# Reordering VectorE's steps in the loop body of a two-layer transformer block: three moves in a table

## The reference

```
x = x + L0_attn(layernorm(x))   # linear attention, 16 heads: phi(q) (phi(k)^T v) Wo, phi = silu + 1
x = x + L0_ffn(layernorm(x))    # 256 -> 2 x 1024, silu gate; 1024 -> 1024 gelu; 1024 -> 1024 gelu; 1024 -> 256
x = x + L1_attn(layernorm(x))   # softmax attention, one head of 256
x = x + L1_ffn(layernorm(x))    # three 256 x 256 products, tanh(h + bias)
```

## Time and profile before

| | |
|---|---|
| median of 3 runs | 2006.14 us (2004.3 to 2007.96) |
| the profiled execution's own time | 2003.38 us |
| its span, first to last instruction | 2001.6 us |
| mean granted clock of TensorE | 0.998 of full speed |
| PE busy | 1914.8 us, 96% of the span |
| DVE busy | 1340.3 us, 67% |
| ACT busy | 782.9 us, 39% |
| POOL busy | 397.6 us, 20% |

### The profile page before, as it was taken

The page is one execution under the profiler, slowest core; times in us unless marked ns, Lnnn a source line. Parts: engine busy times, 40 slices in busy tenths (PEclk is TensorE's granted clock), DMA queues, the critical chain, the costliest instruction groups (busy, mean ns, idle before and its releaser), DMA issues.

```text
span 2001.6 us, 27379 instructions
## 1 busy us (share of the span) xinstructions
PE 1914.8 (96%) x10170; PEld 1634.2 (82%) x10170; DVE 1340.3 (67%) x3183; ACT 782.9 (39%) x1258; POOL 397.6 (20%) x344
## 2 busy tenths in 40 slices
PE   8999999999999999999999999999999999999998
PEld 6888787887878888788787887878788787887886
DVE  6676686766757577676776766758666686765347
ACT  3443434343343433434334343343433434343333
POOL 1212030221302113021130311303022030220211
PEclk9999999999999999999999999999999999999999
DMA  9531312313022130221303113031231312213200
GB/s 370 176 105 43 122 37 74 106 43 137 22 81 99 53 137 22 87 83 53 137 32 106 53 65 125 32 117 42 76 114 43 122 37 74 106 43 127 81 15 23
DMA packets 59241, 171.10 MB, mean 85 GB/s; under 512 B 5296, under 2 KB 25520, under 8 KB 58928
## 3 DMA queue, kind: packets, MB, share of 16 engines
q1 hardware_dynamic: 59104, 169.25, 24.4%
HBM read 160.85 MB, written 19.92 MB: 90 GB/s over the span
## 4 chain that ended last, share of the span: by engine, by line
PE 74%; DVE 16%; ACT 6%; issue 3%; DMA 0%; ACTq 0%; POOL 0%; DVEq 0%
PE ffn_fill L1152 33%; PE att_fill L1083 23%; PE ffn_fill L1083 12%; DVE turned L801 5%; PE ffn_fill L1205 4%; DVE turned_b L818 3%; DVE act_lo L840 2%; DVE xn L720 2%; ACT whole L1013 1%; ACT act_hi L1015 1%; PE att_fill L1283 1%; DVE sm L908 1%; DVE prob_t_lo L903 1%; ACT L1044 1%; ACT L1013 1%
## 5 line engine op out<-in xcount | busy, mean ns | idle before, releaser
L1152 PE MATMUL ffn_fill<-act_hi,hw 128*128 128x512 f32 x2048 | 804.1, 393 | 0.0
L1152 PE MATMUL ffn_fill<-act_lo,hw 128*128 128x512 f32 x2048 | 798.6, 390 | 0.0
L1152 PEld LDWEIGHTS ffn_fill<-act_lo,hw 128*128 128x128 f32 x2048 | 384.7, 188 | 76.7
L1152 PEld LDWEIGHTS ffn_fill<-act_hi,hw 128*128 128x128 f32 x2048 | 384.6, 188 | 76.7
L840 DVE TENSOR_TENSOR act_lo<-whole,act_hi 128x512 fp32r<-128x512 f32 x256 | 177.0, 691 | 280.4 <-ACT act_hi L1015 279.5
L1013 ACT ACTIVATE whole<-ffn_fill,scales 128x512 f32<-128x512 f32 x256 | 175.9, 687 | 467.5 <-PE ffn_fill L1152 467.2
L681 POOL TENSOR_TENSOR act_lo<-whole,act_hi 128x512 fp32r<-128x512 f32 x128 | 166.4, 1300 | 299.9 <-DVE act_hi L836 299.3
L1083 PE MATMUL ffn_fill<-half_hi,w 128*128 128x512 f32 x512 | 203.6, 398 | 2.8 <-DVE wz_lo L946 2.7
L1083 PE MATMUL ffn_fill<-half_lo,w 128*128 128x512 f32 x512 | 200.6, 392 | 0.0
L1015 ACT ACTIVATE act_hi<-whole 128x512 fp32r<-128x512 f32 x256 | 161.7, 631 | 8.2
L818 DVE STREAM_TRANSPOSE turned_b<-xn_b 32x128 f32<-32x128 f32 x480 | 145.1, 302 | 6.6
(11 more groups left out here) (242 smaller groups left out, 3167.5 us busy)
## 6 DMA issues: line engine op xcount, KB each, us to landing
hw<-scratch_h1T SPq DMA_DIRECT2D x128, 512.0 KB, 3.3
hw<-scratch_h2T SPq DMA_DIRECT2D x128, 512.0 KB, 3.2
x<-in_L_attn_x SPq DMA_DIRECT2D x16, 512.0 KB, 4.0
out<-x SPq DMA_DIRECT2D x15, 512.0 KB, 4.0
w<-scratch_w1T SPq DMA_DIRECT2D x1, 1024.0 KB, 8.9
w<-scratch_w2T SPq DMA_DIRECT2D x1, 1024.0 KB, 11.0
w<-scratch_w3T SPq DMA_DIRECT2D x1, 1024.0 KB, 8.5
rows<-in_rows SPq DMA_DIRECT2D x1, 640.0 KB, 5.7
```

What stands on the lines that cost most here:

```text
L1152: last = pe.matmul(bank[:], view(hw[:, j, k, :]), view(moving[:, k, :]), start=k == 0 and half == 0, stop=k == KH - 1 and half == 1)
```

## The change

Three steps change their place in DVE's table for the body. No other engine's table is touched, no instruction is added or removed, and the tables of the first and the last stage stay.

```diff
     "BODY": order_from("""
-         a:AST H5 a:ANO a:Ta H6 a:Tb H7 W0 W1 c:CSTa U0 a:AKV0 U1 a:AKV1 c:CSTb U2 a:AKV2 U3 a:AKV3 U4 U5 a:AS
+         a:AST H5 a:ANO a:Ta H6 H7 a:Tb W0 W1 c:CSTa U0 a:AKV0 U1 a:AKV1 c:CSTb U2 a:AKV2 U3 a:AKV3 U4 U5 a:AS
     a:AQ U6 a:AM U7 c:CNO a:AO n:BST0 c:LT c:CQ G0 n:BST1 c:CV G1 c:CZ c:CS0 G2 c:CS1 c:CP0 c:CS2 c:CO0 c:CP1
-    c:CS3 G3     c:CO1 c:CP2 G4 c:CO2 c:CP3 n:BNO0 c:CO3 c:DSTa c:DSTb G5 c:DNO n:NT0a G6 n:NT0b c:LT G7 n:NTL0
+    c:CS3     c:CO1 c:CP2 G3 G4 c:CO2 c:CP3 n:BNO0 c:CO3 c:DSTa c:DSTb G5 c:DNO n:NT0a G6 c:LT n:NT0b G7 n:NTL0
     n:BNO1     c:CF H0 n:NT1a H1 n:NT1b H2 n:NTL1 H3 H4"""),
```

## The result

| | before | after |
|---|---|---|
| median, device us | 2005.23 (4 runs, 2004.3 to 2007.96) | 1947.22 (4 runs, 1946.51 to 1949.3) |
| ratio to before, 95% interval | | 0.971 [0.9693, 0.9727] |
| the profiled execution's own time | 2003.38 | 1946.51 |
| its span | 2001.6 | 1944.8 |
| mean granted clock | 0.998 | 0.997 |

The account below looks back on a forecast made before the run. TensorE was busy 96%, so time could come only from its idle gaps: 1.2 + 0.63 + 2.05 = 3.9 us in each of 14 passes, 54 us, giving 2006.1 - 54 = 1952 us; range 1938 to 1967.

Parts of the forecast that it names:

- Site 3: CF's wait for LT's low half: LT ahead of NT0's second half removes it, 2.05 us a pass.
- the cover: At H0's last eighth: G7's delayed low half is still ready 0.64 us before TensorE loads its weights.
- Site 2: CO2's wait for prob_t_lo: G3 behind CO1 and CP2 saves 0.63 us a pass; ACT's high half ends the rest.
- the upper bound of the prediction: At CO2: 1.42 us a pass if ACT's high half were not in the way.
- Site 1: W0's wait for H7's low half: H7 ahead of the second transposes removes 1.92 us, of which 1.2 is kept.
- the prediction's other branch: At line 850: DVE's addition goes between POOL's two instructions, AKV0 loads 0.74 late, 1.08 us is kept.
- debt in the U steps: DVE, held up by POOL, starts U0 only 0.43 us earlier and stays behind TensorE up to AS.
- the test that the prediction names: DVE's start of U0: at 1126 or earlier its first rival holds; beyond 1128 W0's gain is given back.
- its first rival: W0's gain is kept whole, DVE's addition coming up 0.1 us before POOL: 4.6 us a pass, 1942 us, 15%.
- Line 850's longest: Expected sign on DVE: the longest run of W's addition to x stretches to nearly 3 us.

Follow-up runs that it names:

- e4: Changed kernel with G7's low half moved further back on DVE, behind NTL0, BNO1 and CF's evictions; 1952.48 us.
- Move 3 alone: Kernel before with only the second LT moved ahead of NT0's second half on DVE; 1974.74 us.
- e9: Kernel before with H7 ahead of the second transposes, G3's low half behind CO1 and CP2, and 14 unused TensorE products ahead of CF's wait; 1976.98 us.
- e6: Kernel before with H7 ahead of the second half of the transposes and 14 unused TensorE products ahead of CF's wait; 1985.31 us.
- e8: Changed kernel with ACT making CP2's and CP3's high halves ahead of G3's and G4's activations, DVE's table following; 1936.55 us.
- its control: Kernel before, its order kept, with the same 14 unused TensorE products ahead of CF's wait; 2005.16 us.
- e10: Changed kernel with W's result scaled in place in PSUM and added to x from there, in two instructions with one SBUF operand each; 1941.27 us.
- move 1 alone: Kernel before with only H7 moved ahead of the second half of the transposes on DVE; 2003.29 us.
- move 2: Kernel before with only G3's low half moved behind CO1 and CP2 on DVE; 2004.45 us.
- moves 1, 2: Kernel before with H7 ahead of the second transposes and G3's low half behind CO1 and CP2, LT left in place; 1994.11 us.

## Why the prediction was right, step by step

The traces account for the whole gain: 1.37 + 0.64 + 2.05 = 4.06 us a pass, 56.8 in 14 passes; the profiled executions differ by 2003.38 - 1946.51 = 56.9.

**Site 3, forecast 2.05.** Right by its own steps. Measured from the product ahead of CF (1080.73 before, 1050.21 after, 30.52 apart), G7's low half was forecast for 1085.39 and came at 1054.75 + 30.52 = 1085.27; the cover was forecast at 0.64 and is 0.80. e4 shows that both are reckoned 0.23 too short, since they end at the weight load and not at its product: "from there on each further delay costs its own length" holds only beyond about 1.0 us there. Move 3 alone made the pass 2.10 us shorter (120.73 instead of 122.83, from AKV0 to AKV0 as above). Its medians give 31.0 us, 1.6 more than 14 times that; the loops of the two traces do not hold that part.

**Site 2, forecast 0.63.** 0.64 by the waits and by the length of the pass (below), and 0.68 from the 9.5 us by which e9's gain exceeds e6's. That ACT ends what is left was shown by e8: removing it gave 10.7 us, 0.76 a pass, as the upper bound of the prediction (1.42 - 0.63 = 0.79) said.

**Site 1, forecast 1.2.** The sum is near (1.37 by the trace, 1.42 by e6 against its control), but one step failed: "It then ends at 1124.13 + 0.56 = 1124.69", DVE standing still until POOL's pair is done. Put into the time of before by H7's low half (1116.53 - 1083.95 = 32.58):

| step | forecast | measured |
|---|---|---|
| POOL's pair starts | 1121.59 | 1121.59 |
| line 850 comes up | 1121.7 | 1121.74 |
| line 850 ends | 1124.69 | 1123.43 |
| POOL's pair ends | 1124.13 | 1124.58 |
| U0's product on DVE | 1127.09 | 1125.84 |

Up to the addition all is within 0.04 us. Then it went as in the prediction's other branch: DVE's addition got in between POOL's two instructions. DVE has no debt in the U steps, and AS does not wait, where 0.3 to 0.5 had been expected. POOL instead is late: AKV0's product comes 0.45 late and its next follows after 0.33 instead of 0.23, so 1.92 - 0.55 = 1.37 is kept; 1.08 had been worked out for this branch, because POOL's second was reckoned 0.58 late and was 0.45, and because the lateness was counted at AKV0's weight load, which before stands 0.22 ahead of its product (1125.95 and 1126.17).

That the sum came near is in part luck: 0.68 was to be lost by DVE's debt at AS, and 0.55 was lost by POOL at AKV0.

My reading of the earlier trace rows, that DVE waits for the whole pair, was wrong: there the addition came up behind the start of POOL's second instruction (1121.22 against 1121.39), and that is the one it waited for. The Trainium skill's rule ("SBUF — State Buffer", "Who interferes with whom") is an exclusive lock, held for one instruction. The traces agree: the same second instruction takes 1.28 us ahead of DVE's addition and 1.74 us behind it. The same section says that a DVE instruction with at most one SBUF input, outside the 2-port perf modes, does not contend with GpSimd. e10 agrees, with 2.55 us for POOL's pair where it had been 2.99.

By the test that the prediction names, DVE's start of U0 (1125.84, before 1126), its first rival would hold; it does not, since the 0.55 moved to AKV0, which that rival left out. Line 850's longest did not reach 3 us; the median of 0.93 is W1's addition, which POOL's second instruction holds up as well (1091.63 to 1092.56, 0.56 behind POOL's end):

```profile
L850 DVE TENSOR_TENSOR x<-x,gated x32: 693/928/1697, 139.2 to 1884.0; 128x512 f32<-128x512 f32 x32
```

**What the prediction did not see.** It held that time can come only from TensorE's idle gaps, and added the three sites as if each could be had by itself. But the same products can also take longer: with move 1 alone PE's busy time rose by 18.4 us. Together the three add; moves 1 and 2, each alone, are worth next to nothing as long as CF's gap is there, because the clock drops behind it, and both together 10.6 us of their 28. With a price of 1.59 a drop the numbers agree (us; the last two columns are median lengths of a pass in the profiled execution, from AKV0's first product to that of the next pass):

| kernel | drops | expected from waits less drops | measured | pass without a drop | with a drop |
|---|---|---|---|---|---|
| before | 0 | | | 122.83 | |
| move 1 | 12 | 19.2 - 19.1 = 0.1 | 2.4 | 121.47 | 123.01 |
| move 2 | 5 | 9.0 - 8.0 = 1.0 | 1.3 | 122.19 | 123.76 |
| moves 1, 2 | 11 | 28.1 - 17.5 = 10.6 | 10.6 | 120.84 | 122.41 |
| move 1, gap filled | 0 | 19.2 | 19.4 | 121.50 | |
| moves 1, 2, gap filled | 0 | 28.1 | 28.9 | 120.83 | |
| after | 0 | 56.8 | 58.0 | 118.73 | |

The passes show it without any sum. In a pass without a drop each move has its whole gain, gap or no gap: 1.36 for move 1, 0.64 for move 2, 1.99 for both. A pass with a drop is 1.54 to 1.57 us longer, and with move 1 alone longer than a pass of before.

The drops are counted in one profiled execution of each kernel. The mean granted clocks of the other runs are like those of the profiled ones: 0.985 to 0.988 with move 1, 0.990 to 0.994 with move 2, 0.986 to 0.988 with both, 0.994 and above in all other kernels. The sum held because move 3 was among the three, and that is luck: the prediction had no term for the clock.

## What to carry to other kernels

When an engine is nearly always busy, follow each of its waits to the work of the releasing engine that nobody needs yet, move that work behind, and then reckon what the moved work makes late, up to the first reader that has no slack. Before a move that measured nothing is thrown away, compare the mean granted clock, the busy time of the same number of products and the length of single passes: a gain may be there and be eaten behind a gap that another move would close. Where DVE and GpSimd both read two operands from SBUF at the same time, ask which instruction of a back-to-back series the other gets in front of, not only whether they collide.

## What the runs showed of the hardware that was not expected

- An idle gap of TensorE of 1.8 us, in a loop that is busy 96% or 97%, was followed by some 3.4 us at half clock (1.2 instead of 2.4 GHz) in 12, 5 and 11 of 14 passes of three kernels, at 1.54 to 1.59 us each, and in none of the 14 passes of the kernel before, which has the same gap and, elsewhere in the pass, one or two more than they. Filling the gap with products removed the drops. What decides, at the same gap in the same kernel (1.79 and 1.80 us), whether the clock drops was not settled. The order is a regular one: with moves 1 and 2, three passes in a row have a drop and the fourth has none, all through the loop. The three kernels with drops differ from before in having less idle time elsewhere and in the length of a pass.
- A weight load that came 0.50 us late made its product only 0.27 us late, since in a run of products it stands 0.23 ahead of its own.
- DVE's addition with two SBUF operands, held up by GpSimd's first instruction, runs before GpSimd's second: 1.69 us instead of 0.69 for DVE, and 2.99 instead of 2.54 for GpSimd's pair. With one of DVE's operands in PSUM, POOL's pair takes 2.55 us and neither is held up.
